# Causal mask on VectorE, one mask product on TensorE, and a step order turned by a quarter in two slotted attentions

## The chip, the core and the metric

The kernel runs on one core of one Trainium2 chip. The metric is the device time of one execution in microseconds (us). A run before the change takes 941.11 us (median of 3 runs, 940.72 to 942.71).

## What is computed

A decoder of two layers for 4 sequences of 256 tokens and width 128: in layer 0 a causal self-attention with 16 heads of 8, a cross-attention, and a block with a second self-attention of 16 heads without a mask and a mixture of experts; in layer 1 a causal attention with clipping, a cross-attention and a mixture. The change touches the first two self-attentions. The first is, cut to what matters:

```python
q, k, v = split(lora_linear(layernorm(x), w_attn, b_attn, la_attn, lb_attn))
att = jnp.einsum('bhqd,bhkd->bhqk', q, k) * (1.0 / np.sqrt(HD))
att = jnp.where(causal[None, None], att, -jnp.inf)
att = jax.nn.softmax(att, axis=-1)
y = jnp.einsum('bhqk,bhkd->bhqd', att, v)
```

The second is the same without the line on `causal`.

## The kernel before, in words

Every engine has its own list of instructions, written out by hand and run strictly in order; semaphores tie the lists together. The class `Slotted` names the semaphores of the two self-attentions: `att0` (the first, causal) and `att1` (the second, no mask). The same code writes both; `a.causal` tells them apart.

The 64 units (4 sequences times 16 heads) are worked in 16 groups (H) of four heads (HG). A group's loop turn is `it`, a head's **step** in it is `j` = 0 to 3, and a unit's number is n = 4 it + j. What a unit n and a group g go through:

1. `fill_slots(g)` (PE, 4 products): spreads the group's queries and keys. ACT copies them (`empty_slots`), POOL makes four key tiles `kz` (`place_keys`).
2. `scores(n)` (PE): queries by keys, two halves of 128 queries, into one of three PSUM banks. With the mask, the first half has 128 keys, the second 256, and after each a bf16 product (line 601) adds the mask on the diagonal block.
3. `maxima(n)` (DVE): the maximum of each row, negated. Line 1611 without a mask, 1608 and 1609 with it. `scores(n)` waits until `maxima(n-3)` has emptied its bank.
4. `split_maxima(g)` (POOL), then `maxima_turned(g)` (PE, line 648, two transposes), then `shifted_queries(g)` (DVE, line 1620): writes `qs`, the group's queries with the maxima in them. It increments `qs_ready`.
5. `shifted(m)` (PE, line 617): keys by `qs`, that is the transposed scores with the maxima taken off, and with the mask a bf16 product (line 620) after each half. It comes LAG = 8 units after `scores`, and the first unit of a group waits for `qs_ready`. ACT takes exponentials (line 1249).
6. `weighted(g)` (PE, line 635, 16 small products): exponentials by values. ACT copies the result (`empty_weighted`, line 1257), PE turns it back (`back_to_tokens(g)`, line 659), DVE divides (`divided(g)`, lines 1629 and 1633). Every fourth group `result_turned` (PE, line 666) turns a finished sequence.

The order in one loop turn before, by steps: PE has `weighted(it-3)` in step 0, `result_turned` in step 1, `maxima_turned(it-1)` and `back_to_tokens(it-3)` in step 2, `fill_slots(it+2)` in step 3, each behind the step's `scores(n)` and `shifted(n-8)`. DVE has `shifted_queries(it-1)` behind the maxima of step 2 and `divided(it-3)` behind those of step 3. `maxima_turned(g)` also waits for ACT's copy of `weighted(g-2)`.

At the end of DVE's turns 2, 4, 6 and 8 of att0 stand asides (`measure`, `scale`): layer norm of the cross-attention's context (lines 1542, 1545, 1559). The mask comes to the chip in `pack_a`, as do ident and the first weights; 128 of its columns are the mask.

Of the kernel before, what the change touches and what calls it, by code (L numbers as in the profile page):

```python
# [29 lines left out]
SHIFT = 3 * HD  # L30
LAG = 8
SCORE_BANKS = (2, 1, 0)
# [31 lines left out]
LAYOUT = {  # L64
    "a": [("ident", P), ("headmask", H), ("slot", HG), ("shift", HG), ("causal", P), ("la0", D), ("lb0", 3 * D), ("w0", 3 * D),
          ("bq0", 1), ("bk0", 1), ("bv0", D)],
# [36 lines left out]
def decoder(nc, x_d, ctx_d, mask_d, packs_d, w1_d, w2_d, iota_d, out_d):  # L103
# [4 lines left out]
    with ctx:  # L108
# [113 lines left out]
        nm = area(2, 2, HG)  # L222
        rec = area(2, 2 * HG)

        area = Area()
# [286 lines left out]
        def _(pe):  # L512
# [49 lines left out]
            def slotted(a, src, name, w, wp, aside=None):  # L562
# [25 lines left out]
                def scores(n):  # L588

                    a.wait(pe, "kz_ready", n + 1)  # L590
                    if n == 2:
                        a.wait(pe, "v_ready", 2)
                    if n >= 3:
                        a.wait(pe, "max_ready", n - 2)
                    out, held, keys_of = bank[SCORE_BANKS[n % 3]], slots[:, n // HG % 3, 0:T], kz[:, n % (4 * HG), :]
                    for u in range(2):
                        keys = P if a.causal and u == 0 else T
                        last = mm(out[:, u * T:u * T + keys], held[:, u * P:(u + 1) * P], keys_of[:, 0:keys],  # L598
                                  start=True, stop=not a.causal)
                        if a.causal:  # L600
                            last = mm(out[:, u * T + keys - P:u * T + keys], identb[:, :], causalb[:, :], start=False, stop=True)
                    last.then_inc(a.shared["score_psum"], 1)

                def shifted(m):
# [9 lines left out]
                    for k in range(2):  # L614
                        later = P if a.causal and k else 0
                        at = k * T
                        last = mm(out[:, at:at + T - later], keys_of[:, k * P:(k + 1) * P], queries[:, later:T],  # L617
                                  start=True, stop=not a.causal)
                        if a.causal:
                            last = mm(out[:, at:at + P], causalb[:, :], identb[:, :], start=False, stop=True)  # L620
                    last.then_inc(a.shared["st_psum"], 1)
# [68 lines left out]
                for it in range(H + 4):  # L690
                    for j in range(HG):
# [3 lines left out]
                        if LAG <= n < LAG + H * HG:  # L695
                            shifted(n - LAG)
                        if j == 0 and 0 <= it - 3 < H:
                            weighted(it - 3)
                        if j == 1 and it >= 7 and (it - 7) % G == 0:
                            result_turned((it - 7) // G)  # L700
                        if j == 1 and it == 1 and aside:

                            a.wait(pe, "v_ready", 1)
                            aside()
                        if j == 2 and 0 <= it - 1 < H:
                            maxima_turned(it - 1)
                        if j == 2 and 0 <= it - 3 < H:
                            if it == 3 and aside:
# [502 lines left out]
        def _(act):  # L1211
# [13 lines left out]
            def slotted(a, g, b, bias_q, bias_k):  # L1225
# [46 lines left out]
                for it in range(H + 4):  # L1272
                    for j in range(HG):
# [3 lines left out]
                        if j == 0 and 2 <= it + 1 < H:  # L1277
                            empty_slots(it + 1)
                        if j == 1 and 0 <= it - 3 < H:
                            empty_weighted(it - 3)  # L1280
                        if j == 1 and it >= 7 and (it - 7) % G == 0:
                            result_ready((it - 7) // G)
# [187 lines left out]
            def context_operands():  # L1470
                activation(laterb[:, :], col("a", "causal"), ACT.Copy, scale=-1.0).then_inc(constants, 1)
                act.wait_ge(sf["w1_split"], 1 + SORTED)
# [38 lines left out]
            activation(identb[:, :], ident, ACT.Copy).then_inc(constants, 1)  # L1511
            activation(causalb[:, :], col("a", "causal"), ACT.Copy).then_inc(constants, 1)
            act.wait_ge(constants, CONSTANTS)
# [14 lines left out]
        def _(dve):  # L1528
# [50 lines left out]
            def slotted(a, bias_q, bias_k, bias_v, asides):  # L1579
# [20 lines left out]
                def maxima(n):  # L1600
# [6 lines left out]
                    if a.causal:  # L1607
                        v.tensor_reduce(nm[:, group % 2, 0, j:j + 1], scores[:, 0:P], AX.X, ALU.max, negate=True)
                        last = v.tensor_reduce(nm[:, group % 2, 1, j:j + 1], scores[:, T:2 * T], AX.X, ALU.max, negate=True)
                    else:  # L1610
# [33 lines left out]
                values(1)  # L1644
                for it in range(H + 3):
                    for j in range(HG):
                        if it < H:
                            maxima(HG * it + j)
                        if j == 2 and 0 <= it - 1 < H:
                            shifted_queries(it - 1)  # L1650
                        if j == 3 and 0 <= it - 3 < H:
                            divided(it - 3)
                    aside(it)
# [235 lines left out]
            def experts():  # L1889
# [22 lines left out]
                v.tensor_copy(onesb[:, :], ones[:, 0:P])  # L1912
                v.tensor_scalar(before_of[:, :], col("a", "causal"), 0.0, None, ALU.is_lt)
                v.memset(pickb[:, NT, :], 0.0)
# [393 lines left out]
def _arrange(inputs):  # L2308
# [28 lines left out]
    def pairs(w):  # L2337
# [7 lines left out]
        "headmask": (np.arange(P)[:, None] // HD == np.arange(H)[None]).astype(np.float32),  # L2345
        "causal": np.where(np.arange(P)[None] <= np.arange(P)[:, None], 0.0, MASKED).astype(np.float32),
        "la0": rows(f("L0_attn_la_attn")), "lb0": rows(f("L0_attn_lb_attn").T), "w0": f("L0_attn_w_attn").T,
# [55 lines left out]
```

## Time and profile before

| | |
|---|---|
| median of 3 runs | 941.11 us |
| the profiled execution | 941.59 us |
| its span, first to last instruction | 939.7 us |
| busy in the span | PE 847.7, DVE 561.1, ACT 480.4, POOL 256.1 us |
| att0 (from the first scores to the projection) | about 24 to 117 us |
| att1 | about 571 to 651 us |

Busy time is summed over stages with different limits. What a change in these two stages does is read from their own timeline: which wait ends last in one group's turn, and how long a turn is. In the timeline a line's first number is the start in us from the span's start, the second the length; PE's products overlap, so their spacing from start to start is what they cost, not their length.

### The profile page before, as it was taken

Reading aid. Unit: us, or ns where it says so; the run is one execution under the profiler, and the core shown is the slowest. Engines: PE = TensorE matmul, PEld = TensorE weight load, DVE = VectorE, ACT = ScalarE, POOL = GpSimd, SP = SyncE. Lnnn points to the kernel's source line nnn. Section 1 sums busy time; section 2 is a strip of 40 time slices with the busy share of each in tenths; the row PEclk is TensorE's granted clock in tenths of the full one; section 3 lists DMA queues with packets and bytes.
Section 4 is the critical chain, followed back from the end, with each engine's and each line's share of the span. In section 5 each row is a group of like instructions: output and inputs, shape, how many; then the busy total and the mean of one; then the engine's idle time right before and its main releaser. Section 6 shows DMA issues by size and latency. Waiting matters only on the chain.

```text
span 939.7 us, 19518 instructions
## 1 busy us (share of the span) xinstructions
PE 847.7 (90%) x6498; PEld 695.7 (74%) x6498; DVE 561.1 (60%) x1561; ACT 480.4 (51%) x1154; POOL 256.1 (27%) x541
## 2 busy tenths in 40 slices
PE   5999879999999999999999968885897888887788
PEld 3888668888888888888888756663796566665565
DVE  3876466555655566655655347774544577666474
ACT  2455465555555555555555315664464476677141
POOL 3864120000000000000000047551075577776110
PEclk9999999999999999999999989999899899999995
DMA  7000000000000000000000030001222000000000
GB/s 270 2 2 1 1 1 1 1 1 1 0 0 0 0 0 0 0 0 0 0 0 0 1 115 1 2 1 28 88 47 59 1 1 0 0 0 0 24 1 22
DMA packets 9410, 15.85 MB, mean 17 GB/s; under 512 B 816, under 2 KB 5040, under 8 KB 8976
## 3 DMA queue, kind: packets, MB, share of 16 engines
q1 hardware_dynamic: 8400, 13.23, 4.2%
q0 software_dynamic: 960, 1.97, 0.9%
q8 instruction: 30, 0.49, 0.2%
q14 instruction: 20, 0.16, 0.1%
HBM read 13.16 MB, written 2.03 MB: 16 GB/s over the span
## 4 chain that ended last, share of the span: by engine, by line
PE 76%; ACT 7%; DVE 6%; issue 6%; POOL 3%; DMA 1%; ACTq 1%; DVEq 0%; POOLq 0%; SPq 0%
PE psum L875 9%; PE psum L887 9%; PE psum L855 5%; PE psum L856 5%; PE psum L857 5%; PE psum L847 5%; PE psum L598 4%; ACT arena L1301 4%; PE psum L840 3%; PE psum L617 3%; PE psum L635 3%; PE psum L956 2%; PE psum L566 1%; PE psum L1034 1%; PE psum L648 1%
## 5 line engine op out<-in xcount | busy, mean ns | idle before, releaser
L1818 DVE TENSOR_REDUCE xnegmax<-psum 128x1 f32<-128x768 f32 x128 | 122.4, 956 | 139.5 <-PE psum L857 139.3
L1405 ACT ACTIVATE arena<-psum,xnegmax 128x768 f32<-128x768 f32 x128 | 115.5, 903 | 139.5 <-DVE xnegmax L1818 97.8
L2265 POOL COPY acur<-A_all 128x128 f32 (+1 forms) x18 | 5.2, 293 | 388.1 <-PE psum L840 388.1
L875 PE MATMUL psum<-pack_a,arena 128*128 128x128 f32 x768 | 106.8, 275 | 0.2 <-ACT arena L1396 0.2
L1249 ACT ACTIVATE arena<-psum 128x384 f32<-128x384 f32 (+1 forms) x128 | 69.5, 546 | 71.2 <-PE psum L620 42.1
L855 PE MATMUL psum<-kv_high,xq_high 128*128 128x384 f32 x256 | 101.5, 396 | 1.8 <-DVE kv_low L1813 1.6
L875 PEld LDWEIGHTS psum<-pack_a,arena 128*128 128x128 f32 x768 | 87.5, 141 | 13.9 <-issue 12.3
L1396 ACT ACTIVATE arena<-psum 128x512 f32<-128x512 f32 x128 | 75.9, 593 | 42.5 <-PE psum L875 42.5
L887 PE MATMUL psum<-arena,xv 128*64 128x256 f32 x768 | 89.9, 383 | 0.0
L856 PE MATMUL psum<-kv_low,xq_high 128*128 128x384 f32 x256 | 86.8, 339 | 0.0
L857 PE MATMUL psum<-kv_high,xq_low 128*128 128x384 f32 x256 | 86.7, 339 | 0.0
L2179 POOL TENSOR_SCALAR kz<-slots,pack_a 128x256 fp32r<-128x256 f32 x128 | 69.4, 557 | 47.8 <-ACT slots L1240 47.8
L1301 ACT ACTIVATE arena<-arena 128x256 f32<-128x256 f32 x128 | 63.6, 498 | 35.8 <-POOL arena L2228 34.1
L887 PEld LDWEIGHTS psum<-arena,xv 128*64 128x64 f32 x768 | 52.3, 137 | 31.0 <-issue 6.0
L598 PE MATMUL psum<-kz,slots 128*128 128x256 f32 (+1 forms) x256 | 62.8, 317 | 0.8 <-POOL kz L2179 0.4
L617 PE MATMUL psum<-qs,kz 128*128 128x256 f32 (+1 forms) x256 | 60.7, 311 | 0.2 <-DVE qs L1620 0.2
L743 PE MATMUL psum<-arena 128*128 (+2 forms) x256 | 59.3, 342 | 0.0
L847 PEld LDWEIGHTS psum<-pack_v,kvT 128*128 128x128 f32 x396 | 54.6, 193 | 2.7 <-DVE xv L1823 0.9
L847 PE MATMUL psum<-pack_v,kvT 128*128 (+1 forms) x396 | 55.5, 277 | 0.7 <-DVE xv L1823 0.7
L855 PEld LDWEIGHTS psum<-kv_high,xq_high 128*128 128x128 f32 x256 | 48.5, 189 | 5.6 <-issue 1.8
L763 PE MATMUL psum<-pack_a,arena 128*128 128x128 f32 x256 | 39.1, 277 | 14.7 <-ACT arena L1311 13.5
L598 PEld LDWEIGHTS psum<-kz,slots 128*128 128x128 f32 x256 | 43.7, 193 | 10.1 <-issue 8.9
(309 smaller groups left out, 1853.6 us busy)
## 6 DMA issues: line engine op xcount, KB each, us to landing
w1all<-in_w SPq DMA_DIRECT2D x1, 2048.0 KB, 8.2
arena<-in_w SPq DMA_DIRECT2D x1, 2048.0 KB, 10.8
pack_v<-in_pack_v SPq DMA_DIRECT2D x1, 1088.0 KB, 9.0
pack_l<-in_pack_l SPq DMA_DIRECT2D x1, 1079.5 KB, 12.0
pack_q<-in_pack_q SPq DMA_DIRECT2D x1, 1024.0 KB, 6.9
pack_a<-in_pack_a SPq DMA_DIRECT2D x1, 653.0 KB, 6.1
pack_f<-in_pack_f SPq DMA_DIRECT2D x1, 556.0 KB, 9.9
x<-in_x SPq DMA_DIRECT2D x2, 256.0 KB, 3.0
```

Source lines behind the costliest of these rows:

```text
L598: last = mm(out[:, u * T:u * T + keys], held[:, u * P:(u + 1) * P], keys_of[:, 0:keys], start=True, stop=not a.causal)
L617: last = mm(out[:, at:at + T - later], keys_of[:, k * P:(k + 1) * P], queries[:, later:T], start=True, stop=not a.causal)
L847: last = mm(bank[7][:, k * P:(k + 1) * P], kvT[:, b, kt * P:(kt + 1) * P], wv[:, bass.ds(it * P, P)], start=True, stop=True)
L855: mm(out, xq_high[:, u % 2, tile], kv_high[:, u // 2, keys], start=True, stop=False)
L856: mm(out, xq_high[:, u % 2, tile], kv_low[:, u // 2, keys], start=False, stop=False)
L857: last = mm(out, xq_low[:, u % 2, tile], kv_high[:, u // 2, keys], start=False, stop=True)
L875: last = transpose(bank[4 + (3 * u + c) % 2][:, (2 * i + h) * P:(2 * i + h + 1) * P], xprob[:, u % 2, h * KEYS + kt * P:h * KEYS + (kt + 1 ...
L887: mm(bank[6][XD * a:XD * (a + 1), 0:T], xv[:, b, kt * P + XD * a:kt * P + XD * (a + 1)], xpT[:, b % 2, a, kt * T:(kt + 1) * T], start=(kt ...
L1301: last = activation(prob[:, j, u, :], limited[:, j, u, :], ACT.Exp, bias=negmax[:, j, u:u + 1], scale=-1.0, accum_out=sums[:, it, u * HG + ...
L1396: activation(xpT[:, (mu // 2) % 2, mu % 2, 2 * c * T:2 * (c + 1) * T], bank[4 + (3 * mu + c) % 2][:, :], ACT.Copy).then_inc(sx["pT_act"], 1)
L1405: activation(xprob[:, u % 2, half * KEYS:(half + 1) * KEYS].rearrange("p (c w) -> p c w", c=2), src, ACT.Exp, bias=xnegmax[:, u % 2, half: ...
L1818: v.tensor_reduce(xnegmax[:, u % 2, half:half + 1], banks_pair(half), AX.XY, ALU.max, negate=True)\
```

## The change

LAG becomes 9. In att0 `maxima` becomes two passes that read the scores from PSUM and the mask from SBUF, add them, write the sum to a scratch tile nobody reads (`unread`) and keep the negated maximum; the mask products behind `scores` go. In `shifted` the two mask products become one of 256 columns into both halves. The mask in `pack_a` grows from 128 to 256 columns. In both attentions the steps of PE and ACT move by one (`weighted`, `result_turned`, `maxima_turned`, `back_to_tokens`, `empty_weighted`, `result_ready`), `fill_slots` stays in step 3. On DVE `shifted_queries` moves from step 2 of turn g+1 to step 0 of turn g+2, `divided` from step 3 of turn g+3 to step 0 of turn g+4.

```diff
-LAG = 8
+LAG = 9
...
-    "a": [("ident", P), ("headmask", H), ("slot", HG), ("shift", HG), ("causal", P), ("la0", D), ("lb0", 3 * D), ("w0", 3 * D),
+    "a": [("ident", P), ("headmask", H), ("slot", HG), ("shift", HG), ("causal", T), ("la0", D), ("lb0", 3 * D), ("w0", 3 * D),
...
                         last = mm(out[:, u * T:u * T + keys], held[:, u * P:(u + 1) * P], keys_of[:, 0:keys],
-                                  start=True, stop=not a.causal)
-                        if a.causal:
-                            last = mm(out[:, u * T + keys - P:u * T + keys], identb[:, :], causalb[:, :], start=False, stop=True)
+                                  start=True, stop=True)
...
-                                  start=True, stop=not a.causal)
-                        if a.causal:
-                            last = mm(out[:, at:at + P], causalb[:, :], identb[:, :], start=False, stop=True)
+                                  start=not (a.causal and k), stop=not a.causal)
+                    if a.causal:
+
+                        last = mm(out.rearrange("p (k t) -> p k t", k=2)[:, :, 0:P], causalb[:, :],
+                                  identb[:, :].unsqueeze(1).broadcast_to([P, 2, P]), start=False, stop=True)
...
-                        if j == 0 and 0 <= it - 3 < H:
+                        if j == 1 and 0 <= it - 3 < H:
                             weighted(it - 3)
-                        if j == 1 and it >= 7 and (it - 7) % G == 0:
+                        if j == 2 and it >= 7 and (it - 7) % G == 0:
                             result_turned((it - 7) // G)
...
-                        if j == 2 and 0 <= it - 1 < H:
+                        if j == 3 and 0 <= it - 1 < H:
                             maxima_turned(it - 1)
-                        if j == 2 and 0 <= it - 3 < H:
+                        if j == 3 and 0 <= it - 3 < H:
...
-                        if j == 1 and 0 <= it - 3 < H:
+                        if j == 2 and 0 <= it - 3 < H:
                             empty_weighted(it - 3)
-                        if j == 1 and it >= 7 and (it - 7) % G == 0:
+                        if j == 2 and it >= 7 and (it - 7) % G == 0:
                             result_ready((it - 7) // G)
...
-                        v.tensor_reduce(nm[:, group % 2, 0, j:j + 1], scores[:, 0:P], AX.X, ALU.max, negate=True)
-                        last = v.tensor_reduce(nm[:, group % 2, 1, j:j + 1], scores[:, T:2 * T], AX.X, ALU.max, negate=True)
+                        if n >= 4:
+                            a.wait(dve, "max_ready", n - 3)
+                        for u in range(2):
+                            keys = T if u else P
+                            last = v.tensor_tensor_reduce(unread[:, n % 4, u * P:u * P + keys], scores[:, u * T:u * T + keys],
+                                                          col("a", "causal")[:, T - keys:T], -1.0, -MASKED, ALU.add, ALU.min,
+                                                          nm[:, group % 2, u, j:j + 1])
...
-                for it in range(H + 3):
+                for it in range(H + 4):
                     for j in range(HG):
                         if it < H:
                             maxima(HG * it + j)
-                        if j == 2 and 0 <= it - 1 < H:
-                            shifted_queries(it - 1)
-                        if j == 3 and 0 <= it - 3 < H:
-                            divided(it - 3)
+                        if j == 0 and 0 <= it - 2 < H:
+                            shifted_queries(it - 2)
+                        if j == 0 and 0 <= it - 4 < H:
+                            divided(it - 4)
                     aside(it)
```

How the instructions stand, at three places. First, DVE in att1, one turn of the loop before (1611 maxima, 1620 `qs`, 1629 and 1633 the division):

```order
L1611 TENSOR_REDUCE arena<-psum 128x2 [waits slotted_nm_ready,slotted_score_psum]
L1611 TENSOR_REDUCE arena<-psum 128x2 [waits slotted_score_psum] x2
L1620 TENSOR_TENSOR qs<-psum,slots 128x256 [waits slotted_st_psum,slotted_mT_psum]
L1611 TENSOR_REDUCE arena<-psum 128x2 [waits slotted_score_psum]
L1629 RECIPROCAL arena<-psum 128x8 [waits slotted_back_psum]
L1633 TENSOR_TENSOR arena<-psum,arena 128x2x32 [waits dve_chain]
```

And one turn in the changed kernel (1617 maxima, 1626 `qs`, 1635 and 1639 the division):

```order
L1617 TENSOR_REDUCE arena<-psum 128x2 [waits slotted_nm_ready,slotted_score_psum]
L1626 TENSOR_TENSOR qs<-psum,slots 128x256 [waits slotted_st_psum,slotted_mT_psum]
L1635 RECIPROCAL arena<-psum 128x8 [waits slotted_back_psum]
L1639 TENSOR_TENSOR arena<-psum,arena 128x2x32 [waits dve_chain]
L1617 TENSOR_REDUCE arena<-psum 128x2 [waits slotted_score_psum] x3
```

The write of `qs` of a group now stands behind the maxima of step 0 of the turn two groups on; before it stood behind those of step 2 of the turn one group on.

Second, PE in att0 from step 0 of a turn to the weighted values, before (598 scores, 617 transposed scores, 601 and 620 mask products, 635 weighted values):

```order
L598 MATMUL psum<-kz,slots 128x128 [waits slotted_max_ready,slotted_kz_ready]
L601 MATMUL psum<-causalb,identb 128x128
L598 MATMUL psum<-kz,slots 128x256
L601 MATMUL psum<-causalb,identb 128x128
L617 MATMUL psum<-qs,kz 128x256 [waits slotted_exp_done,slotted_qs_ready]
L620 MATMUL psum<-identb,causalb 128x128
L617 MATMUL psum<-qs,kz 128x128
L620 MATMUL psum<-identb,causalb 128x128
L635 MATMUL psum<-arena 9x256 [waits slotted_qs_ready,slotted_yraw_ready,slotted_exp_done]
```

And in the changed kernel (599 scores, 616 transposed scores, 620 the mask product, 636 weighted values), from step 0:

```order
L599 MATMUL psum<-kz,slots 128x128 [waits slotted_max_ready,slotted_kz_ready]
L599 MATMUL psum<-kz,slots 128x256
L616 MATMUL psum<-qs,kz 128x256 [waits slotted_exp_done]
L616 MATMUL psum<-qs,kz 128x128
L620 MATMUL psum<-identb,causalb 128x2x128
L599 MATMUL psum<-kz,slots 128x128 [waits slotted_max_ready,slotted_kz_ready]
L599 MATMUL psum<-kz,slots 128x256
L616 MATMUL psum<-qs,kz 128x256 [waits slotted_exp_done,slotted_qs_ready]
L616 MATMUL psum<-qs,kz 128x128
L620 MATMUL psum<-identb,causalb 128x2x128
L636 MATMUL psum<-arena 9x256 [waits slotted_qs_ready,slotted_yraw_ready,slotted_exp_done]
```

A step of four large and four mask products has become four large and one; the wait for `qs_ready` stands in step 1, one step after the scores whose maxima DVE takes ahead of that `qs`.

Third, DVE in att0 in the changed kernel, step 0 of a turn (1613 a masked pass and behind each the row that stores its result, 1626 `qs`):

```order
L1613 ISA arena<-psum,pack_a 128x128 [waits slotted_max_ready,slotted_nm_ready,slotted_score_psum]
L1613 ISA arena 128x1
L1613 ISA arena<-psum,pack_a 128x256
L1613 ISA arena 128x1
L1626 TENSOR_TENSOR qs<-psum,slots 128x256 [waits slotted_st_psum,slotted_mT_psum]
L1635 RECIPROCAL arena<-psum 128x8 [waits slotted_back_psum]
L1639 TENSOR_TENSOR arena<-psum,arena 128x2x32 [waits dve_chain]
```

Two reductions a unit have become two passes with a store of one column each.

## Rows read from the trace of the kernel before

**Rows 1.** Time windows: us, busy time per engine (instructions), granted clock, DMA share, GB/s

```profile
57.00:68.00 11.00, 10.97 (x122) 9.15 (x114) 8.41 (x35) 5.76 (x15) 7.61 (x16) 1.00 0.01 3
...
594.00:613.00 19.00, 17.08 (x165) 13.08 (x164) 13.47 (x28) 12.48 (x26) 10.30 (x25) 1.00 0.00 1
...
110.00:116.00 6.00, 3.72 (x42) 2.25 (x34) 2.71 (x13) 2.20 (x6) 1.27 (x2) 1.00 0.01 3
...
550.00:555.00 5.00, 2.37 (x6) 1.41 (x7) 2.64 (x12) 0.78 (x1) 4.62 (x7) 0.69 0.01 3
```

**Rows 2.** Chain that ended last, in att0: start us, us, what

```profile
67.54 0.77 PE psum L635 x16
...
73.01 0.77 PE psum L635 x16
```

**Rows 3.** Timeline of att0, PE: start us, us, engine, line, operation, tiles, shape

```profile
66.57 0.22 PE L598 MATMUL psum<-kz,slots 128*128 128x128 f32 x1
66.63 0.23 PE L601 MATMUL psum<-causalb,identb 128*128 128x128 bf16 x1
...
69.13 0.31 PE L598 MATMUL psum<-kz,slots 128*128 128x128 f32 x1
69.28 0.23 PE L601 MATMUL psum<-causalb,identb 128*128 128x128 bf16 x1
69.33 0.36 PE L598 MATMUL psum<-kz,slots 128*128 128x256 f32 x1
69.53 0.23 PE L601 MATMUL psum<-causalb,identb 128*128 128x128 bf16 x1
69.57 0.36 PE L617 MATMUL psum<-qs,kz 128*128 128x256 f32 x1
```

**Rows 4.** Timeline of att0, DVE: maxima back to back, then the write of qs

```profile
69.31 0.28 DVE L1608 TENSOR_REDUCE arena<-psum 128x1 f32<-128x128 f32 x1
69.51 0.41 DVE L1609 TENSOR_REDUCE arena<-psum 128x1 f32<-128x256 f32 x1
69.84 0.28 DVE L1608 TENSOR_REDUCE arena<-psum 128x1 f32<-128x128 f32 x1
...
70.67 0.42 DVE L1620 TENSOR_TENSOR qs<-psum,slots 128x256 fp32r<-128x256 f32 x1 [0.22 <-PE psum L648]
```

**Rows 5.** Timeline of the third attention, DVE: passes that also keep a maximum

```profile
769.80 0.29 DVE L1701 TENSOR_SCALAR_CACHE_REDUCE arena<-psum 128x128 f32<-128x128 f32 x1
...
770.36 0.08 DVE L1701 DVE_READ_ACCUMULATOR arena<-psum 128x1 f32 x1
770.36 0.29 DVE L1701 TENSOR_SCALAR_CACHE_REDUCE arena<-psum 128x128 f32<-128x128 f32 x1
```

**Rows 6.** Timeline of att1, PE, DVE and ACT in one turn

```profile
610.97 0.50 PE L598 MATMUL psum<-kz,slots 128*128 128x256 f32 x2
...
611.31 0.39 PE L617 MATMUL psum<-qs,kz 128*128 128x256 f32 x2
...
611.51 1.29 DVE L1611 TENSOR_REDUCE arena<-psum 128x2 f32<-128x512 f32 x2 [0.92 <-PE psum L598]
...
612.23 0.38 ACT L1257 ACTIVATE arena<-psum 128x256 f32<-128x256 f32 x1
...
612.71 0.41 PE L648 MATMUL psum<-pack_a,arena 128*128 128x128 f32 x2 [0.53 <-issue]
...
615.68 0.50 PE L598 MATMUL psum<-kz,slots 128*128 128x256 f32 x2
```

**Rows 7.** Timeline of att0, DVE: two of the four asides

```profile
55.65 0.86 DVE L1542 BATCH_NORM_STATS2 moments<-ctx_x 128x6 f32<-128x128 f32 x4
...
57.72 0.38 DVE L1545 BATCH_NORM_AGGREGATE stat<-moments 128x2 f32<-128x6 f32 x4
...
66.72 2.14 DVE L1559 TENSOR_SCALAR ctx_z<-ctx_x,stat 128x128 f32<-128x128 f32 x8
```

**Rows 8.** DMA issues: tile, queue, count, size, us to landing

```profile
pack_a<-in_pack_a SPq DMA_DIRECT2D x1, 653.0 KB, 6.1
```

More of the change, by code:

```diff
@@ L223, in decoder @@
         rec = area(2, 2 * HG)
+        unread = area(4, T + P)
         area = Area()
@@ L1470, in context_operands @@
             def context_operands():
-                activation(laterb[:, :], col("a", "causal"), ACT.Copy, scale=-1.0).then_inc(constants, 1)
+                activation(laterb[:, :], col("a", "causal")[:, P:T], ACT.Copy, scale=-1.0).then_inc(constants, 1)
                 act.wait_ge(sf["w1_split"], 1 + SORTED)
@@ L1511, in _ @@
             activation(identb[:, :], ident, ACT.Copy).then_inc(constants, 1)
-            activation(causalb[:, :], col("a", "causal"), ACT.Copy).then_inc(constants, 1)
+            activation(causalb[:, :], col("a", "causal")[:, P:T], ACT.Copy).then_inc(constants, 1)
             act.wait_ge(constants, CONSTANTS)
@@ L1912, in experts @@
                 v.tensor_copy(onesb[:, :], ones[:, 0:P])
-                v.tensor_scalar(before_of[:, :], col("a", "causal"), 0.0, None, ALU.is_lt)
+                v.tensor_scalar(before_of[:, :], col("a", "causal")[:, P:T], 0.0, None, ALU.is_lt)
                 v.memset(pickb[:, NT, :], 0.0)
@@ L2345, in _arrange @@
         "headmask": (np.arange(P)[:, None] // HD == np.arange(H)[None]).astype(np.float32),
-        "causal": np.where(np.arange(P)[None] <= np.arange(P)[:, None], 0.0, MASKED).astype(np.float32),
+        "causal": np.where(np.arange(T)[None] - P <= np.arange(P)[:, None], 0.0, MASKED).astype(np.float32),
         "la0": rows(f("L0_attn_la_attn")), "lb0": rows(f("L0_attn_lb_attn").T), "w0": f("L0_attn_w_attn").T,
```

## The prediction

> **What bounds the kernel now.** The change touches two stages, so I read the windows first, by stage. In att0 PE is busy for 10.97 of 11.00 us and VectorE (DVE) for 8.41; in att1 PE for 17.08 of 19.00 us and DVE for 13.47; the granted clock is full in both [rows 1]. PE sets att0. In att1 it has a hole, so the next view is the chain of waits for the turn's length, and then the timeline, to see what stands in a turn.
>
> A turn of four heads in att0 takes 73.01 - 67.54 = 5.47 us on the chain [rows 2], in att1 615.68 - 610.97 = 4.71 us [rows 6].
>
> Inside an att0 step the spacing of PE's starts is the price. A scores product of 128 columns behind a mask product takes 69.28 - 69.13 = 0.15, its mask product 0.05, the 256-column one 0.20, its mask product 0.04 [rows 3]. The other half of the step has the same shapes, so a step is 2 x 0.44 = 0.88 us. A float32 product behind another one is far cheaper: 128 columns took 66.63 - 66.57 = 0.06 [rows 3], and two of 256 columns show 0.39 from first start to last end, where two starting together would show about 0.28, so 0.12 apart (estimate from [rows 6], where the four products of a step fill 0.47). The mask products thus cost little themselves; what they cost is that each float32 product behind one is 0.09 dearer.
>
> In att1 PE's hole is the 0.53 us ahead of the turned maxima at 612.71. ScalarE's copy of the weighted values ends at 612.23 + 0.38 = 612.61, and PE starts 0.10 later [rows 6]: that is what PE waited for. DVE is idle for 0.92 us before the first maximum of that stretch [rows 6]; it is no bound there, it follows PE.
>
> **Part 1, the products.** A changed step has scores of 128 and 256 columns, transposed scores of 256 and 128, and one mask product of 256. By the spacings above: 0.15 (behind a mask product) + 0.12 + 0.12 + 0.06 = 0.45, and the mask product. No row shows a 256-column one in bf16. Below it is 0.04, what the 128-column one takes; above 0.20, the float32 one [rows 3]. I take 0.10, twice the narrow one, to which it is nearest. A step becomes 0.55 (0.49 to 0.65), 0.33 less, a turn 1.32 less: 5.47 would become 4.15 if PE alone set it.
>
> **Part 2, DVE's masked passes.** Back to back, the reductions of a unit start 69.84 - 69.31 = 0.53 us apart per unit [rows 4]. The nearest relative of the new pass is the one of the third attention, which also reads PSUM, writes a tile and stores a column: 770.36 - 769.80 = 0.56 per unit of the same two widths, the 0.08 store of the column inside that [rows 5]. I take 0.56. The bounds: below 0.53 (a plain reduction); above 1.1, an addition and a reduction each at the reduction's price. The wait for its own `max_ready` is on a maximum three units back and costs nothing.
>
> The Trainium skill (VectorE: DVE Perf Modes, "The DRAIN you can't avoid") speaks against this part: it says that after every VectorE operation the next cannot issue until the pipe is empty, though it excepts operations that are not held. By the strict form a unit would be 0.29 + 0.42 and two stores of 0.08, 0.87 us. Here the reduction at 69.31 runs for 0.28 and the next starts at 69.51 [rows 4], so the trace does not agree with it, and I keep 0.56; the other value is priced with the first rival.
>
> **Part 3, the turned steps.** This decides. `qs` of group g now stands in DVE's list behind the maxima of unit 4g+8, the first scores of a turn. PE needs `qs` for `shifted(4g)`, directly behind the scores of unit 4g+9, one step later. DVE strictly follows its list, so it cannot write `qs` earlier although the turned maxima have long been there. Before, that write stood two steps earlier and was done by the time PE came to it.
>
> In att1, from PE's first scores product of the turn: the second product starts 0.12 later, runs 0.28 and reaches DVE 0.04 later (611.47 to 611.51 [rows 6]), 0.44. The reduction holds DVE for 0.60 (two show 1.29, one is 0.69 long, so they start 0.60 apart [rows 6]), the `qs` pass is 0.43 long (0.42 to 0.43 [rows 4]), and PE starts 0.10 after its releaser [rows 6]. Sum 1.57. Meanwhile PE has six products of 0.12, 0.70. It then waits 0.87 us, with `weighted`, the next scores and the transposed scores all queued behind. The wait ahead of the turned maxima does not shrink in exchange: it runs from `weighted` and a `shifted` behind it, which move with the held product. Fourteen groups (0 to 13) have such a maximum ahead of `qs`: 14 x 0.87 = 12.2. At the start the turned maxima of the first groups come a step later and wait less for POOL; I take off 1.0 (estimate, about one such wait). Att1: **+11.2**.
>
> In att0 the chain is 0.06 + 0.28 + 0.04 = 0.38, passes 0.56, `qs` 0.43, 0.10: 1.47. PE has 0.06 + 0.12 (scores behind a float32 fill), 0.12 + 0.06 + 0.10, and 0.15 + 0.12, in all 0.73. It waits 0.74. Ahead of the turned maxima: in att1 it is 612.71 - 611.31 = 1.40 from the start of a `shifted` to them [rows 6]; with att0's narrower exponential some 0.1 less, 1.3, of which PE now fills 0.28 + 0.27 + 0.28 = 0.83. So 0.47 there, where PE's dense timeline of before has room for 0.2. The turn: 4.15 + 0.74 + 0.27 = 5.16, that is 0.31 less, x 14 = -4.3.
>
> The asides lose their cover. They used to run in DVE's idle time; now each stands between the last maxima of a turn and the first of the next, ahead of a `qs` that PE waits for. DVE's idle time there is about 1.4: its passes and side work fill 4 x 0.56 + 0.43 + 0.4 = 3.1 of 5.16, and the last pass of a turn ends soon after its scores. A scale takes 2.14, a measure 58.10 - 55.65 = 2.45 [rows 7]: 2 x 0.7 + 2 x 1.05 = +3.5. Att0: **-0.8**.
>
> **Part 4, the rest.** `pack_a` grows by 64 KB of 653, landing in 6.1 us at the head of the chain [rows 8]: between 0 and 0.6 in proportion, I take 0.3. POOL's key tiles and its split of the maxima only get more time. DMA queues are not passed.
>
> Sum: 11.2 - 0.8 + 0.3 = +10.7. On the profiled execution's 941.59 that is 952.3; the median of the runs is 0.5 below that execution, so **951.8 us**. Differences within 0.2% (1.9 us) count as none, about what a measurement of this kernel can tell from no change.
>
> **The rivals.** (a) The masked pass is dear, 1.1 per unit. Then att0's wait grows by 0.54, a turn is 5.70, and DVE has so little idle time (4 x 1.1 + 0.83 of 5.70) that the asides come through nearly whole, 4.3 + 4.9 less 2: att0 is 14 x 0.23 + 7 = +10, in all 963. For it: no row shows this very operation. Against: its relative in rows 5. By the skill's strict rule above, 0.87 per unit, it would be 14 x 0.31 more, with the asides some 1 more: 957. Of the chance of (a) that reading has 0.03.
>
> (b) The other side, faster: `qs` is not late. It decides at 0.70 us: were the reduction and the `qs` pass both done in the time of PE's six products, att1 would stay and att0's turn be 4.15 + 0.27 = 4.42, 14 x -1.05 = -14.7: 927. For it: PE really saves 1.3 a turn. Against: the pass and the write of `qs` alone are 1.03 in att1 and 0.99 in att0.
>
> (c) The new wait swallows the old one: PE's hole ahead of the turned maxima closes by what `qs` takes. Then att1 is 14 x (0.87 - 0.53) - 1 = +3.8 and att0 14 x -0.78 + 3.5 = -7.4, in all 938, or with half of it 945. For it: both are waits on a loop. Against: the copy that PE waits for stands behind a `shifted` that the new wait holds.
>
> (d) The waits lower TensorE's clock. In att1 PE's busy share falls from 0.90 to about 17.08 / 22.5 = 0.76; a stretch at 3.72 of 6.00 (0.62) kept the full clock, one at 2.37 of 5.00 had 0.69 of it [rows 1]. At 1.2 GHz a turn's 3.9 us of products would double; a few turns so give 963 or more.
>
> **How the numbers follow.** The forecast with its own bounds (mask product, passes, 0.7 to 1.0 for the wait in att1, asides) reaches from 946 to 957: 0.72. (a) 0.10, (b) 0.05, (c) 0.08, (d) 0.05. The range from 944 to 963 takes in half of (c) and most of (a). Faster: (b) and part of (c), 0.09. Within 0.2%: 0.03. Slower: 0.88.
>
> **What would show it.** Right: in att1 a turn near 5.6, PE idle near 0.85 ahead of the transposed scores of step 1 with the `qs` write as its releaser, and DVE idle before the first maxima of a turn and then writing `qs`; in att0 a step of 0.55, a turn of 5.1 to 5.2, and turns with an aside longer by 0.7 to 1.1. Wrong: a turn of att1 still 4.7; masked passes spaced over 0.7 a unit; a step of att0 still above 0.7; a clock below 1.00 in either stage.

## The result and the profile after

The change made the kernel slower. Its median is 957.21 us (4 runs, 955.32 to 960.12); the kernel before took 941.63 (4 runs, 940.72 to 942.71) beside it. The ratio is 1.0168, with a 95% interval from 1.0135 to 1.0201, so 15.6 us more. The forecast was 951.8, in a range from 944 to 963. One run of the kernel before (2044 us) and one of the turned steps alone (2780 us) were slow throughout and are left out of all times below.

The profiled execution of the changed kernel is the longest of its four runs, 960.12 us, with a span of 958.3. I cut both traces at the same places and read each stage's length and the spacing of the turns from the starts of `weighted` (us):

| | before | after | difference |
|---|---|---|---|
| start, to the first projection | 13.18 | 13.91 | +0.7 |
| att0, from there to the cross-attention | 104.17 | 106.33 | +2.2 |
| of it, from the last `weighted` to the end | 4.34 | 5.47 | +1.1 |
| between, to the projections of att1 | 436.23 | 438.43 | +2.2 |
| att1 | 97.06 | 109.31 | +12.3 |
| after att1 | 289.11 | 290.31 | +1.2 |
| a turn of att0 without an aside | 5.47 | 5.37 | -0.10 |
| a turn of att1 | 4.71 | 5.61 | +0.90 |

Work is not what grew: over the span PE is busy for 842.7 us, 5.0 less than before, and DVE for 559.9, 1.2 less. What grew is waiting.

The rows behind that, first by window, as in [rows 1], of the changed kernel: a stretch of att0, one of att1, and one around att0's end. Columns are us, busy time of PE, PE's loads, DVE, ACT and POOL (instructions), granted clock, DMA share and GB/s.

```profile
57.00:79.00 22.00, 17.04 (x171) 13.27 (x170) 15.11 (x90) 10.99 (x25) 12.75 (x28) 1.00 0.01 2
...
580.00:620.00 40.00, 32.02 (x287) 23.62 (x287) 23.79 (x49) 22.75 (x46) 21.61 (x48) 1.00 0.01 1
...
117.00:124.00 7.00, 6.41 (x43) 5.57 (x43) 3.15 (x15) 1.47 (x3) 1.45 (x3) 0.51 0.01 2
```

In both stretches of the attentions the clock is full. In att0 PE, which was busy for 10.97 of 11.00 us before, is now busy for 17.04 of 22.00: it no longer sets that stage. In att1 its share falls from 0.90 to 32.02 / 40 = 0.80. The last row is a second matter: a stretch that takes in the last 3 us of att0, which ends at 120.25, and goes on behind it ran at the half level, 1.2 GHz, as did another from 134 to 141. Before, the first of them had the full clock (same columns):

```profile
117.00:124.00 7.00, 5.69 (x60) 4.62 (x59) 4.93 (x21) 4.89 (x10) 3.87 (x10) 1.00 0.00 1
```

Over the span 79.9 us are at the half level after the change and 56.8 before. The changed stages and the start give 0.7 + 2.2 + 12.3 = 15.2 of the span's +18.6; the other 3.4 lies in stages whose code is the same, and 1.1 of the 15.2 in the end of att0, where the clock is half (rival (d) below).

The chain of waits of the changed kernel (start us, us, what) in att0, to hold beside [rows 2], and in att1:

```profile
76.11 0.77 PE psum L636 x16
...
80.52 0.35 DVE qs L1626
...
81.48 0.77 PE psum L636 x16
```

```profile
599.35 0.42 DVE qs L1626
...
600.32 0.98 PE psum L636 x16
...
605.93 0.98 PE psum L636 x16
```

`qs` (line 1626, before 1620) now stands on the chain once for each of the groups 0 to 13, in both attentions; before it stands there nowhere. The turn is 81.48 - 76.11 = 5.37 in att0 and 605.93 - 600.32 = 5.61 in att1.

The timeline of one turn of att1 in the changed kernel, which answers to [rows 6] (start, length, engine, line, shape; in brackets an idle time and what ended it):

```profile
598.31 0.40 PE L599 MATMUL psum<-kz,slots 128*128 128x256 f32 x2
...
598.74 0.69 DVE L1617 TENSOR_REDUCE arena<-psum 128x2 f32<-128x512 f32 x1 [1.29 <-PE psum L599]
598.78 0.40 PE L599 MATMUL psum<-kz,slots 128*128 128x256 f32 x2
...
599.35 0.41 DVE L1626 TENSOR_TENSOR qs<-psum,slots 128x256 fp32r<-128x256 f32 x1
...
599.82 0.50 PE L616 MATMUL psum<-qs,kz 128*128 128x256 f32 x2 [0.64 <-DVE qs L1626]
...
602.98 0.41 PE L649 MATMUL psum<-pack_a,arena 128*128 128x128 f32 x2 [0.53 <-issue]
```

DVE has been idle for 1.29 us when the first scores of the turn come. It reduces them first and writes `qs` at 599.35, and only then does PE start the transposed scores of step 1, at 599.82. From the first scores that is 1.51 us, for which 1.57 was forecast. PE's last product before the wait starts near 598.78 + 0.12 = 598.90, so the spacing is 0.92, of which one product's 0.12 is work: some 0.80 lost, of which the row shows 0.64 as idle because the products overlap. The two products behind the wait take 0.43 from their start to `weighted` (599.82 to 600.25) where they took 0.33 before (614.37 to 614.70); with that 0.10 the turn is 0.90 longer. The old wait of 0.53 ahead of the turned maxima is still there, in full.

The same for att0, which answers to [rows 3, 4]:

```profile
84.92 0.39 PE L599 MATMUL psum<-kz,slots 128*128 128x128 f32 x2
85.15 0.34 PE L616 MATMUL psum<-qs,kz 128*128 128x256 f32 x2
85.33 0.28 PE L620 MATMUL psum<-identb,causalb 128*128 128x256 bf16 x1
85.35 0.29 DVE L1613 CUSTOM_DVE_ANT_0 arena<-psum,pack_a 128x128 f32<-128x128 f32 x1 [1.24 <-PE psum L599]
85.37 0.48 PE L599 MATMUL psum<-kz,slots 128*128 128x128 f32 x2
...
85.57 0.42 DVE L1613 CUSTOM_DVE_ANT_0 arena<-psum,pack_a 128x256 f32<-128x256 f32 x1
...
85.91 0.42 DVE L1626 TENSOR_TENSOR qs<-psum,slots 128x256 fp32r<-128x256 f32 x1
86.39 0.45 PE L616 MATMUL psum<-qs,kz 128*128 128x256 f32 x2 [0.54 <-DVE qs L1626]
86.67 0.28 PE L620 MATMUL psum<-identb,causalb 128*128 128x256 bf16 x1
86.89 0.40 PE L636 MATMUL psum<-arena 128*9 128x256 f32 x4
```

The two masked passes of a unit and the write of `qs` start at 85.35, 85.57 and 85.91: 0.56 a unit. The joined mask product takes 85.37 - 85.33 = 0.04. From the first scores to the held product it is 86.39 - 84.92 = 1.47.

### The profile page after: what moved, and what is told of

Same layout as the page of the kernel before. It is cut to its first block, busy times and chain, and to the rows that moved or that the text cites. A ratio compares the mean times of both kernels' runs of the same rounds, so it can differ in the third digit from the quotient of the medians.

```text
span 958.3 us, 19308 instructions
## 1 busy us (share of the span) xinstructions
PE 842.7 (88%) x6306; PEld 685.9 (72%) x6306; DVE 559.9 (58%) x1689; ACT 479.9 (50%) x1154; POOL 256.3 (27%) x541
## 4 chain that ended last, share of the span: by engine, by line
PE 73%; DVE 9%; ACT 7%; issue 7%; POOL 2%; DMA 1%; ACTq 1%; DVEq 1%; SPq 0%; POOLq 0%
PE psum L876 9%; PE psum L888 9%; PE psum L856 5%; PE psum L857 5%; PE psum L858 5%; PE psum L848 5%; ACT arena L1302 4%; PE psum L841 3%; PE psum L636 3%; PE psum L616 3%; PE psum L599 3%; PE psum L957 2%; PE psum L1035 2%; PE psum L567 1%; PE psum L1045 1%
## 5 line engine op out<-in xcount | busy, mean ns | idle before, releaser
L876 PE MATMUL psum<-pack_a,arena 128*128 128x128 f32 x768 | 106.8, 275 | 0.2 <-ACT arena L1397 0.2
L876 PEld LDWEIGHTS psum<-pack_a,arena 128*128 128x128 f32 x768 | 87.4, 141 | 13.9 <-issue 12.3
L616 PE MATMUL psum<-qs,kz 128*128 128x256 f32 (+1 forms) x256 | 50.9, 284 | 21.1 <-DVE qs L1626 21.1
L1617 DVE TENSOR_REDUCE arena<-psum 128x2 f32<-128x512 f32 x64 | 42.4, 687 | 29.7 <-PE psum L599 29.7
L616 PEld LDWEIGHTS psum<-qs,kz 128*128 128x128 f32 x256 | 38.9, 189 | 28.5 <-DVE qs L1626 26.9
L599 PE MATMUL psum<-kz,slots 128*128 128x256 f32 (+1 forms) x256 | 56.2, 305 | 1.3 <-DVE arena L1596 0.8
L1613 DVE CUSTOM_DVE_ANT_0 arena<-psum,pack_a 128x128 f32<-128x128 f32 (+1 forms) x128 | 39.1, 352 | 24.3 <-PE psum L599 23.9
```

What stands on the lines that cost most here:

```text
L876: last = transpose(bank[4 + (3 * u + c) % 2][:, (2 * i + h) * P:(2 * i + h + 1) * P], xprob[:, u % 2, h * KEYS + kt * P:h * KEYS + (kt + 1 ...
```

## The experiments

Eight kernels were run in two sets, each with the kernel before beside it on the same chip (medians 942.5 and 942.41 us). None leaves out a part of the computation.

### The masks without the turned steps

The change as it is, but with LAG 8 and every step of PE, ACT and DVE where it was before:

```diff
-LAG = 9
+LAG = 8
...
-                        if j == 0 and 0 <= it - 2 < H:
-                            shifted_queries(it - 2)
-                        if j == 0 and 0 <= it - 4 < H:
-                            divided(it - 4)
+                        if j == 2 and 0 <= it - 1 < H:
+                            shifted_queries(it - 1)
+                        if j == 3 and 0 <= it - 3 < H:
+                            divided(it - 3)
```

> The change's mask part with the old order of steps (LAG 8, all steps as before). Theory 1 (the late qs write of the turned steps costs the time, the mask part saves): att1's turn stays at 4.71 us, att0's turn falls from 5.47 to 4.4 (a step of 0.55, no wait for qs), the asides stay covered; att0 shorter by about 12, 0.7 lost to the larger pack_a, 930 in all. Theory 2 (the masked pass on DVE is what costs): att0's turn stays above 5.2 and the time at 941 or more.

Measured: 929.99 us (928.99 to 931.51), ratio 0.9853 [0.9793, 0.9914]. The masks alone are a gain of 12.5 us. Att0 is 91.29 us long, 12.9 shorter; att1 is 97.75, 0.7 longer, with the turns of before, 4.71. Its chain in att0, then its timeline of PE:

```profile
73.94 0.77 PE psum L636 x16
...
78.50 0.77 PE psum L636 x16
```

```profile
71.24 0.28 PE L620 MATMUL psum<-identb,causalb 128*128 128x256 bf16 x1
71.67 0.41 PE L649 MATMUL psum<-pack_a,arena 128*128 128x128 f32 x2
72.16 0.47 PE L599 MATMUL psum<-kz,slots 128*128 128x128 f32 x2
...
72.69 0.36 PE L585 MATMUL psum<-qk_high,sel 128*128 128x256 f32 x1
```

The turn is 4.56 on the chain, where 4.4 was expected. A step, from its scores to the product behind its mask, is 72.69 - 72.16 = 0.53, where it was 0.88. The rest of the turn's distance to 4.15, which is the prediction's estimate for PE alone, is the gap ahead of the turned maxima: 71.67 - 71.24 = 0.43 where the mask product takes 0.04.

### The turned steps without the masks

Before, with LAG 9 and the steps where the change puts them:

```diff
-LAG = 8
+LAG = 9
...
-                        if j == 2 and 0 <= it - 1 < H:
-                            shifted_queries(it - 1)
-                        if j == 3 and 0 <= it - 3 < H:
-                            divided(it - 3)
+                        if j == 0 and 0 <= it - 2 < H:
+                            shifted_queries(it - 2)
+                        if j == 0 and 0 <= it - 4 < H:
+                            divided(it - 4)
```

> The turned steps alone (LAG 9), masks by TensorE as before. Theory 1: att1 as in the changed kernel, a turn of 5.61 instead of 4.71, 12 us more; att0's turn grows from 5.47 to about 5.9 (a wait for qs of some 0.5, since its steps hold 0.88 of PE's work each), 7 to 9 more with the asides; 961 in all. Theory 2: only att1 is longer, and the whole is 954 or less.

Measured: 973.46 us (three runs, 966.58 to 976.65), ratio 1.0281 [1.0185, 1.0377], of the medians 1.033. Att0 is 10.5 longer and att1 13.0, with turns of 5.85 and 5.61, so the loss is there without any masked pass. The profiled execution took 976.65, because its stretch behind att1 is 9.0 longer too. The window of its last products, and its chain in att0, where the first of the two turns holds an aside (6.49) and the second none (5.84):

```profile
945.00:974.00 29.00, 25.57 (x73) 16.08 (x72) 10.55 (x35) 2.61 (x5) 0.39 (x1) 0.50 0.06 18
```

```profile
69.06 0.77 PE psum L635 x16
...
75.55 0.77 PE psum L635 x16
...
81.39 0.77 PE psum L635 x16
```

The kernel's end ran at half the clock in this profiled execution. It did so once more, in the profiled execution of the joined mask product alone (916 to 946 us), where the stretch behind att1 is 297.2 long; in the other eight traces it is 288.6 to 290.6. Why in these two, the runs don't tell. The three times go with the granted clock of the whole run: 976.65 at 0.950, 973.46 at 0.953, 966.58 at 0.964. The last is near 942.5 + 10.5 + 13.0 = 966.0, what the two stages give, and 5 above the 961 expected.

### The write of qs ahead of the maxima

The changed kernel with one statement of DVE's list moved:

```diff
-                        if it < H:
-                            maxima(HG * it + j)
                         if j == 0 and 0 <= it - 2 < H:
                             shifted_queries(it - 2)
+                        if it < H:
+                            maxima(HG * it + j)
```

> The changed kernel with one line moved: DVE writes qs in step 0 ahead of that step's maxima instead of behind them. Theory 1: the wait for qs ahead of the transposed scores of step 1 goes (0.75 in att0, 0.86 in att1 by the trace of the changed kernel), part of it may come back as a later wait for ScalarE's copy; turns of 4.7 to 4.8 in att0 and 4.7 to 5.1 in att1; 7 to 13 less in att0 and att1 together with each, 941 to 946 in all. Theory 3 (the turned steps cost through another wait, of POOL or ScalarE): the turns stay at 5.3 and 5.6 and the time above 953.

Measured: 939.37 us (10 runs, 938.76 to 949.45), ratio 0.9985 [0.9943, 1.0027]; 941 to 946 was expected. One statement, moved by one place, takes back some 17 us (1.0168 - 0.9985 = 0.0183 of 942), about the whole loss, for the interval takes in 1. Turns are 4.68 in att0 and 4.99 in att1, neither of them what it was in the kernel with the masks alone (4.57 and 4.71). The timeline of its att1 has the reason:

```profile
573.74 0.41 PE L649 MATMUL psum<-pack_a,arena 128*128 128x128 f32 x2 [0.53 <-issue]
574.19 0.42 DVE L1626 TENSOR_TENSOR qs<-psum,slots 128x256 fp32r<-128x256 f32 x1 [0.36 <-PE psum L649]
...
576.01 1.05 PE L636 MATMUL psum<-arena 128*9 128x256 f32 x16 [0.21 <-ACT arena L1250]
```

`qs` is written as soon as the turned maxima are there (574.19 behind 573.74), and PE doesn't wait for it. But the turned steps leave `weighted` waiting 0.21 for ACT's exponentials in every turn, and the 0.53 has not gone. So even where `qs` is early, the turned order costs 0.28 a turn in att1. In att0 it costs 0.11, and the three turns with an aside are still 5.61, 5.74 and 5.66 long: the aside still stands ahead of `qs` in DVE's list, and there alone `qs` is still on the chain in full turns. These costs make most of the distance to the masks alone, 9.4 us.

### The asides behind the held write

The changed kernel, with each aside moved from a turn's end to behind the next turn's `qs` and division:

```diff
                             divided(it - 4)
-                    aside(it)
+                        if j == 0:
+                            aside(it - 1)
```

> The changed kernel with the asides moved behind the qs write and the division of the next turn's step 0. If the asides cost what the prediction says, by standing ahead of a qs that PE waits for, att0's long turns (6.0, 6.3, 6.0 against 5.37) fall to 5.4 and the time by 2 to 3.5; att1 unchanged. If their length on DVE is what costs, the turns stay long and the time the same.

Measured: 954.27 us (953.3 to 954.86), ratio 1.0116 [1.0055, 1.0178]. That is 2.9 less than the change, but from another set, and the interval takes in the change's 1.0168; the times alone don't settle it. Its chain in att0 shows that the turn with an aside is now as long as the next one:

```profile
60.81 0.77 PE psum L636 x16
...
66.10 1.36 DVE ctx_z L1560 x5
...
71.56 0.77 PE psum L636 x16
...
76.93 0.77 PE psum L636 x16
```

From 60.81 to 71.56 there are two turns, 5.38 each, the aside's passes (`ctx_z`) between them. In the changed kernel three of the four aside turns were 6.00, 6.29 and 6.01 long. The first aside stands ahead of the first `weighted` and shows in no turn. It is on the chain of the changed kernel all the same, between the `qs` of the groups 0 and 1 (`moments`); below it is the same place with the asides later:

```profile
29.95 0.35 DVE qs L1626
...
32.38 0.80 DVE moments L1543 x4
...
35.28 0.35 DVE qs L1626
```

```profile
29.17 0.34 DVE qs L1626
...
32.88 0.35 DVE qs L1626
```

The second `qs` comes 5.33 behind the first in the changed kernel and 3.71 here: the first aside costs 1.6. Att0 as a whole is 102.31 long, for 106.33.

### The copy of the weighted values ahead of an exponential

The experiments left the 0.53 us that no kernel so far had lost: PE waits for ACT's copy of the weighted values, and in ACT's list that copy stands behind an exponential of the same step. Here the copy goes ahead of it, once on the masks alone and once on the kernel before:

```diff
                         n = HG * it + j
+                        if j == 1 and 0 <= it - 3 < H:
+                            empty_weighted(it - 3)
                         if LAG <= n < LAG + H * HG:
...
-                        if j == 1 and 0 <= it - 3 < H:
-                            empty_weighted(it - 3)
```

> The mask part with the old steps, and ScalarE copies the weighted values of a turn's step 1 ahead of that step's exponential instead of behind it, in both attentions. Theory 1 goes on: with the mask products gone PE's remaining wait in a turn is the one for this copy (0.39 ahead of the turned maxima in att0, 0.53 in att1). If so, turns of 4.1 to 4.2 in att0 instead of 4.57 and 4.1 to 4.2 in att1 instead of 4.71, 13 to 15 less than the mask part alone, 916 in all. If another engine (DVE's passes, POOL's split) is next in line right behind, the turns stay above 4.4 and 4.5 and the time above 923.

> The kernel before with that one line of ScalarE moved alone. By the same reading att1 falls to the turn of the run with the mask part (the same code there), 4.1 to 4.2, and att0 from 5.47 by no more than its 0.2 of room ahead of the turned maxima, to 5.3: 930 to 932 in all.

Measured: 915.23 us (913.37 to 917.87), ratio 0.9709 [0.9679, 0.9739], with the masks; 928.91 (928.35 to 931.65), ratio 0.9853 [0.9824, 0.9883], on the kernel before. The first beats the kernel before by 27 us and the changed one by 42. The two gains add up: 12.5 for the masks and 13.5 for the copy make 26.0, and 27.2 was measured. In att1 of the kernel with both:

```profile
563.05 0.50 PE L599 MATMUL psum<-kz,slots 128*128 128x256 f32 x2
563.19 0.38 ACT L1258 ACTIVATE arena<-psum 128x256 f32<-128x256 f32 x1
...
564.11 0.38 PE L649 MATMUL psum<-pack_a,arena 128*128 128x128 f32 x2
...
567.03 0.50 PE L599 MATMUL psum<-kz,slots 128*128 128x256 f32 x2
```

The copy is done at 563.57, the exponential comes behind it, and the turned maxima start at 564.11 with no idle time shown. The turn is 567.03 - 563.05 = 3.98, where it was 4.71 and 4.1 to 4.2 was expected. It is 0.73 less, more than the 0.53 that the wait showed as idle, because products overlap: from the turn's first scores to the turned maxima it is now 564.11 - 563.05 = 1.06, for 612.71 - 610.97 = 1.74 before [rows 6]. On the kernel before the copy alone gives the same 3.98 in att1 and 5.23 in att0. With the masks too, the turns of att0 lie between 4.00 and 4.85; what makes the longer ones was not traced.

### The two halves of the mask change, each alone

The kernel before with the joined mask product alone, and the masks alone without the joined product, so with only the masked passes of DVE new:

```diff
-                        if a.causal:
-                            last = mm(out[:, at:at + P], causalb[:, :], identb[:, :], start=False, stop=True)
+                                  start=not (a.causal and k), stop=not a.causal)
+                    if a.causal:
+
+                        last = mm(out.rearrange("p (k t) -> p k t", k=2)[:, :, 0:P], causalb[:, :],
+                                  identb[:, :].unsqueeze(1).broadcast_to([P, 2, P]), start=False, stop=True)
```

> The kernel before, with the two mask products of the transposed scores joined into one of 256 columns and nothing else. By the spacings a float32 product behind a float32 one costs 0.09 less than behind a mask product, and the joined product takes about 0.04: a step of 0.75 instead of 0.88, a turn of 4.95 to 5.1 instead of 5.47, 936 in all, a third to a half of what the mask part brings. Rival: a mask product costs its columns; joining two of 128 into one of 256 saves nothing and the time stays at 941.

> The mask part without the joining: VectorE adds the mask for the maxima, the transposed scores keep a mask product after each half, steps as before. By the spacings a step of about 0.65, 0.1 over the mask part's 0.54: a turn of 4.75 to 4.95, 932 to 935 in all. With theory 2 (the masked pass is dear and only TensorE's joining saves) no better than 941.

Measured: 938.15 us (12 runs, 935.2 to 948.37), ratio 0.9960 [0.9930, 0.9991], for the joined product; 934.14 (931.63 to 934.71), ratio 0.9898 [0.9869, 0.9927], for the masked passes. The chains in att0, of the first and then of the second:

```profile
64.91 0.77 PE psum L637 x16
...
70.09 0.77 PE psum L637 x16
```

```profile
63.59 0.77 PE psum L634 x16
...
68.43 0.77 PE psum L634 x16
```

Turns of 5.18 and 4.84: 0.29 and 0.63 less than before, and 0.91 less with both. They are worth 4.3 and 8.3 us, and 12.5 together: two separate gains, both on PE. For the joined product the turn lies 0.08 above the upper end of what was expected, 5.1, in part for the wider spacing ahead of `weighted`, which is told below. The three longest of its twelve runs, 947.58 to 948.37, had a granted clock of 0.952 to 0.954, the others of 0.961 to 0.970.

## Why the prediction was right, and where it was short

**Direction and mechanism were right.** The forecast's deciding step, that `qs` stands behind a maximum that itself waits for PE, is shown by three things: the releaser on the chain and in the timeline of the changed kernel, the loss in the kernel with the turned steps alone, and its return when one statement is moved.

**Part 1, the products.** The step was forecast at 0.55; 0.53 was measured. The mask product of 256 columns is at the lower bound, 0.04, not at 0.10. The rest of the step is dearer than its sum of 0.45 by 0.04. The spacing ahead of `weighted` was overlooked; it is told below.

**Part 2, the masked passes.** 0.56 a unit, as taken. The Trainium skill (VectorE: DVE Perf Modes, "The DRAIN you can't avoid") would in its strict form have had 0.87; the second pass starts 0.22 after a first one that is 0.29 long, so the strict form does not hold here. The Trainium skill excepts operations that are not held; whether that is the reason no run here shows. Rival (a) falls.

**Part 3, att1.** The wait was forecast at 0.87 and the turn near 5.6; the turn is 5.61, 0.90 more than before. The size is in part luck: the wait is 0.80, and the 0.10 that the products behind it lose was not counted. Stage: +12.3, for +11.2. The step that failed is the 1.0 taken off for the start: 14 x 0.90 = 12.6, so only 0.3 of it came. Rival (c), that the new wait swallows the old one, falls: the 0.53 is there in full [rows 6].

**Part 3, att0.** This is the mis-sized term: -0.8 was forecast, +2.2 came. The chain of 1.47 is exact, but the turn is 5.37 and not 5.16, and three spacings make nearly all of the 0.21. The step with the wait takes 86.67 + 0.04 - 85.37 = 1.34, that is 0.80 more than the 0.54 of a step without one (77.36 to 77.86, and 0.04), for 0.74 forecast. In it the held transposed scores, of 256 and 128 columns, start at 86.39 and their mask product at 86.67: 0.28, where 0.18 was counted and is measured in the step that didn't wait (85.15 to 85.33). The gap ahead of the turned maxima is the largest part. In the changed kernel, then in the kernel before:

```profile
72.49 0.28 PE L620 MATMUL psum<-identb,causalb 128*128 128x256 bf16 x1
73.14 0.41 PE L649 MATMUL psum<-pack_a,arena 128*128 128x128 f32 x2 [0.37 <-issue]
```

```profile
69.96 0.23 PE L620 MATMUL psum<-identb,causalb 128*128 128x128 bf16 x1
70.23 0.41 PE L648 MATMUL psum<-pack_a,arena 128*128 128x128 f32 x2
```

The spacing was 0.27 and is 0.65: 0.38 more, for 0.27 forecast. And `weighted` follows its mask product at 86.89, 0.22 later, where before the change it was 0.16 (72.78 to 72.94): 0.06 that was not counted. This last one doesn't come from the wait. In the kernel with the masks alone the spacing is 0.21 (73.66 to 73.87), with the joined product alone 0.22 (69.81 to 70.03), and with the masked passes alone, which keep the narrow product, 0.16 (73.05 to 73.21). It is the price of a wide mask product ahead of `weighted`, which I had not looked up.

**The asides.** Forecast 2 x 0.7 + 2 x 1.05 = 3.5. The three turns with one are longer by 0.63, 0.92 and 0.64, and the first aside, ahead of the first `weighted`, costs the 1.6 that its experiment showed: 3.8 in all, and moving them away shortens att0 by 4.0 in the two traces. This term was near. Of the +2.2 of att0 the asides are thus 3.8 and the half clock at its end 1.1 (rival (d) below); what is left for the turns is -2.7, in place of the -4.3 forecast.

**Part 4, the larger pack.** The start is 0.7 later, forecast 0.3, but the size is not shown as its cause. The larger pack landed in 6.8 us in the changed kernel and in 6.0 to 7.2 in the five others that have it; the smaller one in 6.1 before [rows 8] and in 5.7 to 6.8 in the three others, 6.8 with the turned steps alone. The spread from run to run is wider than the term, so the runs don't show it.

**Rival (b),** that `qs` is not late, would have given 927. The masks alone, 929.99, show that this price was near: had the order been kept, that is what the change would have been.

**Rival (d), the clock.** It didn't come as told: in the stretches of both attentions shown above the clock was full. But the clock is in the result. The end of att0, from the last `weighted` on, takes 4.34 in the three traces in which the clock is full there (before, and the two with the copy first), and 5.23 to 5.47 in the seven in which a part of it runs at the half level. The stage between the attentions, whose code is the same in all, is 436.2 to 436.3 long in the three traces with 2.5 to 5.6 us at the half level in it, 436.9 to 437.0 in three with 6.8 to 6.9, and 437.9 to 438.4 in four with 7.8 to 11.8. So 1.1 of att0's +2.2 and the +2.2 between go with the clock. The four runs lie between 955.32 and 960.12, wider than those of before, and the two shortest have the highest clock. Whether the changed order of att0 brings the half level on is open: over the span the kernel with later asides, with the same order of products, had 70.1 us of it, that with `qs` first 67.0, the masks alone 73.3, in stretches that lie apart. No experiment was made on the clock alone.

So the sum of +10.7 compares with 15.2 in the stages that it speaks of: 0.4 more at the start, 3.0 in att0, of which 1.1 is the clock, and 1.1 in att1.

## What to carry to other kernels

In lists that are run strictly in order, look at what stands ahead of a write that another engine waits for. If that is a pass which itself waits for the same engine, the two waits run one after the other, once a turn: here 0.9 us on a turn of 4.7, while both engines had idle time. When a wait has stayed the same through several edits, go to its releaser and ask what stands ahead of it in its own list: the copy behind an exponential, moved by one place, was worth as much as all of the mask change. And a mixed change is measured in its parts: here a gain of 12.5 and a loss about twice as large came in one edit.

## What was not expected of the hardware

A bf16 mask product of 256 columns between float32 ones is spaced 0.04 us, no more than one of 128 [rows 3]. Two float32 products behind a wait take 0.28 to the next product, the same two without a wait 0.18. And the time at the half clock differs from one kernel's profiled execution to the next without a change in the code concerned: 56.8 us before, 63.3 to 98.3 in the others, in stretches that move.
